# Last three experts' rows added on TensorE by 0/1 matrices, down products three half jobs behind, norm factors split between VectorE and POOL

## What is computed

```python
cap = int(EXPERT_CAPACITY * T / E)                 # 2.0 * 1024 / 8 = 256 tokens an expert
probs = jax.nn.softmax(scores, axis=-1)            # scores = x @ gate_w, 8 experts
top_p, top_idx = jax.lax.top_k(probs_et, cap)      # each expert picks its 256 tokens
xin = jnp.take_along_axis(x[:, None, :, :], top_idx[..., None], axis=2)
h = jax.nn.gelu(jnp.einsum('BElC,ECH->BElH', xin, w1), approximate=False)
y = jnp.einsum('BElH,EHC->BElC', h, w2) * top_p[..., None]
out = jnp.zeros((B, T, C), x.dtype).at[b_idx, top_idx].add(y)
...
x = _layernorm(x + attention(x)); x = _layernorm(x + ffn(x))
```

## Time and profile before

| | before |
|---|---|
| median of 3 runs | 981.73 us (978.76 to 984.08) |
| the profiled execution's own time | 979.79 us |
| its span, first to last instruction | 978.0 us |
| busy: PE, DVE, ACT, POOL | 89%, 73%, 77%, 68% |
| mean granted TensorE clock | 0.956 of full speed |

### The profile page before, as it was taken

How to read it: one execution, slowest core, us unless ns; L and a number is a source line. 1 busy time by engine, 2 the same in 40 slices (tenths; PEclk the granted TensorE clock), 3 DMA queues, 4 the chain that set the end, 5 groups by cost and what they waited for, 6 DMA issues and landing times.

```text
span 978.0 us, 14970 instructions
## 1 busy us (share of the span) xinstructions
PE 870.7 (89%) x4598; PEld 734.7 (75%) x4598; DVE 714.5 (73%) x1178; ACT 749.4 (77%) x1449; POOL 664.1 (68%) x1055
## 2 busy tenths in 40 slices
PE   6899999999999999999999999999998996676550
PEld 4678888888888888888888888777787775575550
DVE  6777777777777777777777777898888865763341
ACT  4988888888888888888988788877787875533441
POOL 4676767677777677767786667666667666756862
PEclk9999999999999999999999999999999997778875
DMA  6000000000000000001020100000000022422424
GB/s 178 2 27 1 28 1 28 1 27 1 28 1 28 1 27 1 28 1 29 0 72 1 28 2 28 4 28 1 17 1 17 1 71 70 122 23 37 85 24 97
DMA packets 48766, 28.57 MB, mean 29 GB/s; under 512 B 5760, under 2 KB 46752, under 8 KB 48688
## 3 DMA queue, kind: packets, MB, share of 16 engines
q1 hardware_dynamic: 43056, 23.29, 8.3%
q0 software_dynamic: 5632, 4.33, 3.3%
HBM read 21.19 MB, written 6.42 MB: 28 GB/s over the span
## 4 chain that ended last, share of the span: by engine, by line
PE 70%; DVE 9%; issue 8%; ACT 5%; POOL 5%; DMA 2%; SPq 1%; POOLq 0%; ACTq 0%; DVEq 0%
PE t_ps L1353 10%; PE ring_b L1316 6%; PE ring_b L1318 6%; PE ring_b L1317 6%; PE ring_a L1316 5%; PE ring_a L1318 5%; PE ring_a L1317 5%; PE u_ps L1316 5%; PE u_ps L1318 5%; PE u_ps L1317 5%; PE o_ps L1316 2%; DVE negmax L916 2%; PE o_ps L1318 2%; PE o_ps L1317 2%; DVE at_lo L923 2%
## 5 line engine op out<-in xcount | busy, mean ns | idle before, releaser
L545 POOL TENSOR_TENSOR attn<-prob 128x1024 f32<-128x1024 f32 x128 | 308.1, 2407 | 192.0 <-ACT prob L688 183.3
L923 DVE TENSOR_TENSOR at_lo<-t_ps,at_hi 128x512 fp32r<-128x512 f32 x253 | 173.7, 687 | 96.5 <-ACT at_hi L671 96.5
L916 DVE TENSOR_REDUCE negmax<-ring_a 128x1 f32<-128x1024 f32 x128 | 156.5, 1222 | 57.3 <-PE ring_a L1318 55.6
L671 ACT ACTIVATE at_hi<-t_ps 128x512 fp32r<-128x512 f32 x253 | 151.4, 598 | 55.5 <-PE t_ps L1353 54.6
L1353 PE MATMUL t_ps<-ident,attn 128*128 128x128 f32 x1012 | 152.8, 273 | 16.6 <-DVE at_lo L923 16.5
L1353 PEld LDWEIGHTS t_ps<-ident,attn 128*128 128x128 f32 x1012 | 123.8, 140 | 45.8 <-DVE at_lo L923 25.8
L916 DVE TENSOR_REDUCE negmax<-ring_b 128x1 f32<-128x1024 f32 x128 | 155.9, 1218 | 1.9 <-PE ring_b L1318 0.9
L688 ACT ACTIVATE prob<-prob,coef 128x1024 f32<-128x1024 f32 x128 | 147.6, 1154 | 2.6 <-POOL coef L516 2.6
L682 ACT ACTIVATE prob<-ring_a,negmax 128x1024 f32<-128x1024 f32 x128 | 142.8, 1115 | 6.3 <-DVE negmax L916 5.8
L682 ACT ACTIVATE prob<-ring_b,negmax 128x1024 f32<-128x1024 f32 x128 | 142.3, 1111 | 1.2 <-DVE negmax L916 1.2
L1316 PE MATMUL ring_b<-xt_hi,q_hi 128*128 128x512 f32 x256 | 111.5, 436 | 2.2 <-ACT prob L682 2.2
(11 more groups left out here) (377 smaller groups left out, 1846.4 us busy)
## 6 DMA issues: line engine op xcount, KB each, us to landing
wq_s<-in_L_attn_Wq SPq DMA_DIRECT2D x16, 128.0 KB, 2.4
wk_s<-in_L_attn_Wk SPq DMA_DIRECT2D x16, 128.0 KB, 2.6
wv_s<-in_L_attn_Wv SPq DMA_DIRECT2D x16, 128.0 KB, 2.1
wvt_s<-in_L_attn_Wv_T SPq DMA_DIRECT2D x16, 128.0 KB, 2.5
wot_s<-in_L_attn_Wo_T SPq DMA_DIRECT2D x16, 128.0 KB, 2.6
raw_a<-in_L_ffn_w SPq DMA_DIRECT2D x8, 256.0 KB
attn<-in_L_ffn_w SPq DMA_DIRECT2D x8, 256.0 KB
xres<-in_L_attn_X SPq DMA_DIRECT2D x2, 512.0 KB, 8.3
```

What stands on the lines that cost most here:

```text
L545: pool.tensor_tensor(attn[:, t % AB, :], prob[:, t % 2, 1, :], prob[:, t % 2, 0, :], ALU.add).then_inc(attn_ready, 1)
L671: act.activation(at_hi[:, g % 2, half * GT:(half + 1) * GT, c], t_bank(t, half)[:, :].rearrange("p (k q) -> p k q", q=P), ACT.Copy).then_i ...
L916: dve.tensor_reduce(negmax[:, par, m:m + 1], ring[m][:, :], axis=AX.X, op=ALU.max, negate=True).then_inc(negmax_ready, 1)
L923: dve.tensor_tensor(at_lo[:, g % 2, k, c], t_bank(t, half)[:, :].rearrange("p (k q) -> p k q", q=P), at_hi[:, g % 2, k, c].bitcast(F32), A ...
```

## The change

1. **Rows by 0/1 matrices.** For the last three jobs (`MIX = 3`: 13, 14, 15) nothing is scattered. POOL writes the numbers 0 to 1023 into a row (`tok_row`, one iota). DVE turns the three experts' indices into floats (`tok_f`) and compares, six passes of 128 x 1024, so that `one_hot[m][k][slot, token]` is 1 where the slot picked the token. PE's `mix(q)` multiplies these by the scaled rows `y_mix`: 16 f32 matmuls of 128 x 128 a job, all three jobs summed up in four PSUM banks that are free by then.
2. **The end of batch 1.** SP's wait counts only the scatters that are left. DVE first adds the two tables (`add_tables`, without a sum), then what PE summed up (`add_mixed`, with the row sum), two tiles to a bank.
3. **Order in a job.** PE does `down(n-3)` in place of `down(n-2)`, and `rows_out` on odd halves; ACT copies `yt` of job q-2 and rounds the next rows ahead of the Gelus, on even halves; DVE does `xs_lower` ahead of `g_lo` on even halves, and scales on odd halves, ahead of `g_lo`.
4. **Norm factors.** DVE computes variance plus eps in one operation on 4 columns (`ln_vars`), POOL only the power (`ln_pows`), in halves, for all norms but the first. Both norms of the second layer stand behind all jobs on ACT, DVE and POOL.

The core of the diff (declarations and the norm functions cut):

```diff
@@ sync
-                    sp.wait_ge(scattered[n], 16 * CT * E // 2 * (b + 1))
+                    sp.wait_ge(scattered[n], 16 * CT * len([q for q in range(E * (b + 1)) if q % 2 == n and not mixes(q)]))
@@ gpsimd
-            ln_factors(1)
+            ln_pows(1, 0)
+            ln_pows(1, 1)
...
+            pool.wait_ge(w_split, 2 * E)
+            pool.iota(tok_row, pattern=[[1, N]], base=0, channel_multiplier=0).then_inc(row_ready, 1)
             for q in range(5):
                 scatter(q)
...
-            for q in range(E, JOBS):
+            for q in range(E, JOBS - MIX):
                 scatter(q)
-                if q == E + 5:
-                    ln_factors(2)
-            ln_factors(3)
+            for n in range(B, 2 * B):
+                for h in range(2):
+                    ln_pows(n, h)
@@ scalar, ffn(n)
+                if half == 0 and 0 <= q - 2 < JOBS:
+                    act.wait_ge(down_ready, q - 1)
+                    need(act, y_ready, q - 3)
+                    act.activation(yt[q % 2], dn_ps, ACT.Copy).then_inc(yt_copied, 1)
...
-                if half == 1 and 0 < q <= JOBS:
-                    act.wait_ge(down_ready, q)
-                    need(act, y_ready, q - 2)
-                    act.activation(yt[(q - 1) % 2], dn_ps, ACT.Copy).then_inc(yt_copied, 1)
@@ vector
+                dve.tensor_scalar(stat[:, 1, c], stat[:, 0, c], 1.0 / D, EPS, ALU.mult, ALU.add).then_inc(ln_var, 1)
...
+            def add_tables(h):
+                dve.wait_ge(x2_in[1][h], 32)
+                s = slice(QT + h * GT, QT + (h + 1) * GT)
+                dve.tensor_tensor(x1[:, s, :], x1[:, s, :], acc_2[1][:, h * GT:(h + 1) * GT, :],
+                                  ALU.add).then_inc(x2_pre, 1)
+            def add_mixed(h):
+                dve.wait_ge(x2_pre, h + 1)
+                for c in range(h * GT, (h + 1) * GT):
+                    j = QT + c
+                    dve.wait_ge(mixed, c // 2 + 1)
+                    dve.scalar_tensor_tensor(out=x1[:, j, :], in0=mix_home(c), scalar=1.0, in1=x1[:, j, :],
+                                             op0=ALU.mult, op1=ALU.add,
+                                             accum_out=rsum[:, j:j + 1]).then_inc(x2_sum, 1)
...
+                for k in range(CT):
+                    dve.tensor_scalar(one_hot[n][k], tok_row, tok_f[:, k, n:n + 1], None,
+                                      ALU.is_equal).then_inc(hot_ready, 1)
@@ vector, ffn(n): rows of job y = q - 2
+                if half == 1 and 0 <= y < JOBS:
+                    dve.wait_ge(y_ready, y + 1)
+                    if not mixes(y):
+                        need(dve, scattered[y % 2], 16 * CT * (y // 2))
+                    dst = y_mix[y - (JOBS - MIX)] if mixes(y) else yr[y % 2]
@@ tensor
+            def mix(q):
+                m = q - (JOBS - MIX)
+                pe.wait_ge(y_scaled, q + 1)
+                pe.wait_ge(hot_ready, CT * (m + 1))
+                for j in range(QT):
+                    for k in range(CT):
+                        last_m = pe.matmul(mix_home(j), one_hot[m][k][:, j * P:(j + 1) * P].bitcast(F32),
+                                           y_mix[m][:, k, :], start=(m == 0 and k == 0 and j % 2 == 0),
+                                           stop=(m == MIX - 1 and k == CT - 1 and j % 2 == 1))
+                    if m == MIX - 1 and j % 2 == 1:
+                        last_m.then_inc(mixed, 1)
...
-                if half == 0 and 0 <= q - 2 < JOBS:
+                if half == 1 and 0 <= q - 2 < JOBS:
                     rows_out(q - 2)
-                if 0 <= n - 2 < 2 * JOBS:
-                    down(n - 2)
+                if 0 <= n - 3 < 2 * JOBS:
+                    down(n - 3)
...
+                if n == 2 * JOBS:
+                    mix(JOBS - 3)
+                if n == 2 * JOBS + 2:
+                    mix(JOBS - 2)
+            mix(JOBS - 1)
```

More of the change, by code:

```diff
@@ L194, in build @@
               for a in (xg0[:, :], flat[:, 4 * N - E * CT * XW:4 * N])]
+        y_mix = [flat[:, n * CAP:(n + 1) * CAP].rearrange("p (k d) -> p k d", d=D) for n in range(MIX)]
+        tok_row = attn[:, 0, :].bitcast(I32)
+        one_hot = [[xt_hi[:, 0:N], xt_hi[:, N:2 * N]], [xt_lo[:, 0:N], xt_lo[:, N:2 * N]],
+                   [t[:, 1].rearrange("p k n -> p (k n)")[:, 2 * N:3 * N] for t in (at_hi, at_lo)]]
+        tok_f = sb("tok_f", [P, CT, MIX])
         pick = sb("pick", [P, CAP], BF16)
@@ L322, in means, with mixes, mix_home @@
             return sum(len(m) for m in MEANS[:n]) + [hi > c for _, hi in MEANS[n]].index(True) + 1
+        def mixes(q):
+            return q >= JOBS - MIX
+        def mix_home(j):
+            return (t_ps, x_ps, u_ps, o_ps)[j // 2][:, (j % 2) * D:(j % 2 + 1) * D]
         def exists(t):
@@ L846, in _ @@
             signs(1, 1)
-            for n in range(14, 2 * JOBS + 2):
+            for n in range(14, 2 * JOBS + 3):
                 ffn(n)
-                if n == 29:
-                    for c in range(QT):
-                        ln_squares(2, c)
+            for c in range(QT):
+                ln_squares(2, c)
             for c in range(QT):
@@ L1144, in ffn @@
                     xs_lower(E)
+                if half == 0 and q + 1 < JOBS and q + 1 != E:
+                    xs_lower(q + 1)
+                y = q - 2
+                if half == 1 and 0 <= y < JOBS:
[3 more added lines that the diff above has]
+                    dst = y_mix[y - (JOBS - MIX)] if mixes(y) else yr[y % 2]
+                    dve.tensor_tensor(dst, yo_ps.rearrange("p (k d) -> p k d", d=D),
+                                      xg[y // E][:, y % E, :, D + y % E:D + y % E + 1].broadcast_to([P, CT, D]),
+                                      ALU.mult).then_inc(y_scaled, 1)
                 if q < JOBS:
@@ L1292, in _ @@
             indices(1, 1)
-            for n in range(14, 28):
+            mix_tokens()
+            for n in range(14, 2 * JOBS):
                 ffn(n)
-            add_parts(2, 0)
-            add_parts(2, 1)
+                if n in (14, 16, 18):
+                    one_hots((n - 14) // 2)
+            add_parts(0)
             ln_means(2, 0)
+            ffn(2 * JOBS + 1)
+            add_parts(1)
             ln_means(2, 1)
-            for n in range(28, 34):
-                ffn(n)
-            ln_end(2, 0)
-            ln_end(2, 1)
-            ffn(34)
-            for h in range(2):
-                add_parts(3, h)
+            ffn(2 * JOBS + 3)
+            ln_vars(2, 0)
+            ln_vars(2, 1)
+            for h in range(2):
+                ln_end(2, h)
+            for h in range(2):
+                add_tables(h)
+            for h in range(2):
+                add_mixed(h)
                 ln_means(3, h)
+            ln_vars(3, 0)
+            ln_vars(3, 1)
             for h in range(2):
@@ L1653, in _ @@
             counts(1, 1)
-            for n in range(15, 2 * JOBS + 3):
+            for n in range(15, 2 * JOBS + 4):
                 ffn(n)
+                if n == 2 * JOBS:
[3 more added lines that the diff above has]
+            mix(JOBS - 1)
 _INS = ["L0_attn_X", "L0_attn_Wq", "L0_attn_Wk", "L0_attn_Wv", "L0_attn_lambda_q1",
```

63 lines of the change are left out of this document (32 added, 31 removed).

## The result

The changed kernel takes **964.63 us** (median of 4 runs, 963.36 to 965.13) beside 980.62 us (4 runs) for the kernel before: ratio 0.983, 95% interval 0.981 to 0.986. The forecast was 963.0, range 957 to 972, faster.

What follows compares the result with a forecast made beforehand. Bounds before: the threshold search to 876 us, POOL from 888.25 to about 943, then POOL's scatters and the final chain. P 883.9, U 933.4, Y 944.1, plus 15.2 gave span 959.3, 18.7 less: 963.0 us, range 957 to 972.

Steps and rivals of the forecast that it cites:

- P: First gather of batch 1, after the threshold search: forecast at 883.9 us on the span, 888.25 before.
- gain and loss: Before the first gather: search 6.1 us shorter; job 4's scaling behind the indices' first half delays gathers from 888.25 to 890.0.
- The rival that the search would not get shorter: Threshold search keeps its length: first gather 6.1 us later, time 969 us; chance 0.14.
- P to the scatter of job 8: Stretch from batch 1's first gather to job 8's scatter, POOL's list unchanged: 33.7 us.
- U: End of the last `up` on PE: P + 48.7, at worst P + 50.3 at half clock; 49.5 taken, 933.4 us.
- the release by the scatter of job 10: Job 12's scaling on DVE begins when job 10's scatter, started at P + 41.2, has landed 5.4 later: P + 46.6.
- Y: End of job 15's scaling, behind three half `down`, two turnings and two mixes: U plus 10.7, 944.1 us.
- The rival of half clock through the mixes: PE at half clock in mixes and last half `down`: 9 us more, time 972 us; chance 0.12.
- unhidden weights: In the mixes each record waits for its own weight load: 31 us more, time 994 us; chance 0.03.
- The end: From Y to the store's end: 6.0 of DVE work, 5.9 of last sums and norm, 3.3 store, sum 15.2 us.
- The edits without a price: Six DVE comparisons of 0.65 to 1.3 us each, the iota, and batch 1's first norm factors: not priced in the forecast.
- where POOL is late they pay nothing: PE's waits for `yt`, 1.4 us a job, go in the new order, but save no time where POOL is late.

Runs made afterwards that it cites:

- Experiment 5: The changed kernel with job 4's rows scaled ahead of the indices of batch 1: 964.11 us, ratio 0.983 to the kernel before.
- experiment 2: The changed kernel with the old order in a job, 0/1 matrices and new norm factors kept: 972.17 us, ratio 0.992 to the kernel before.
- the change's second trace: The changed kernel run once more, unchanged, in a later group: 964.19 us, ratio 0.984 to the kernel before.
- experiment 1: The changed kernel without 0/1 matrices, all rows scattered, new order and norm factors kept: 968.19 us, ratio 0.989 to the kernel before.
- experiment 4: The changed kernel with the old norm factors, three POOL operations on eight columns: 964.99 us, ratio 0.986 to the kernel before.

## Why the prediction was right, point by point

**P.** Forecast 883.9, measured 885.70. Of the 1.8, 1.0 is the later start of the layer in this execution. The other 0.8 is the search: from the first count to P it took 42.1 for 45.6, so 3.5 less, where gain and loss were put at 6.1 and 1.75. Experiment 5 puts the loss at 2.5, and so the gain at 6.0: the term that was mis-sized is the loss. That the gain comes out so near is partly luck: the first three pairs of rounds gave 4.5 where 5.6 was forecast, and the stretch behind them, to the second half of the indices, 1.4 where 0.5 was. The indices' second half came 1.83 behind the first, where it had been 2.30 (887.26 less 884.96 of the earlier trace rows), and the second DMA of job 4's scatter took 1.75 beside the comparisons: 0.47 and 0.2 more to lose. The pairs of rounds went from 9.1, 7.9 and 8.6 to 8.5, 6.6 and 6.0: 6.0 is the forecast's value at the full clock, now with DVE's own work as the floor. The first pair gained only 0.6; in it `cand` waited for POOL, 0.4 longer than before (last section). The rival that the search would not get shorter falls, and experiment 2 shows that it is the order that shortens it.

**P to the scatter of job 8:** forecast 33.7, measured 34.4, and 33.6 in the change's second trace. POOL bounds it as forecast.

**U.** Job 12's scaling began at P + 47.4 (forecast P + 46.6), and not released by a DMA. The scatter of job 10 began at P + 41.9 in place of 41.2, and by the 5.3 that job 8's took from there it was in at P + 47.2; PE and ACT were a little later still. Nor did this scaling set U, though the forecast had it do so. PE's only wait of size from 922 to 938 us is that for job 10's scaling:

```profile
PE ring_b L1677 <- DVE prob L1205: 4.7, 1, 4.7
```

From its end at 925.98 PE ran through into the mixes, first 4 us at half clock (granted 0.50 to 929.9), then at 1.00; in the 10 us up to P + 51 it is 9.98 busy. So PE's own work behind job 10 is the bound there, and the release by the scatter of job 10 is a step that the forecast had wrong. The last `up` ended at 936.1, P + 50.4, near its worst case, which stood for the half clock, and 0.9 over the value taken.

**Y.** Forecast 10.7 behind U, measured 10.3; a matmul cost 0.22 where I took 0.24, at a granted clock of 1.00, that is the full one. The rival of half clock through the mixes falls, and so does that of unhidden weights, the only one that ended slower.

**The end.** Forecast 15.2, measured 15.2 from Y on. Two small errors cancel in it: the last normalising ended 11.3 behind Y where 11.9 was forecast, and the store took 3.9 in place of 3.3. The rest fits, with powers of 1.05 and 1.01 (forecast 1.0), normalising 2.14 (2.2), table adds 1.29 for two (1.3). The tables were asked for at 940.35, P + 54.7, and nobody waited for them.

The edits without a price: the comparisons took 0.75 each and drew out three issues by 0.9 together; the normalising of batch 1's first norm ended 1.1 us later behind the attention, and the first Gelu still came 4.8 us behind the last attention sum, as before.

**What bounds the kernel before: the step that failed.** The prediction had POOL as the bound from 888.25 to 943 and said of PE's waits for `yt` that "where POOL is late they pay nothing". That holds up to job 10. Behind it the old order was the bound, at 5.4 us a job, and experiment 1 shows the new order with all scatters at 3.6. The forecast time did not suffer, since its Y was built from P upward in the new order and took nothing over from the old stretch; my expectation for experiment 2, which did, missed by 3.

**Sum.** The layer from its first count was forecast at 116.7 and took 118.0. Added last, the matrices give 5.7, the order 7.4 and the factors 0.2 us of the layer, together 13.3 of 17.4. The 0.2 is the least sure: behind Y it is 1.3, and the rest of experiment 4's trace happens to be 1.1 shorter. The remaining 4.1 are shared: both the order and the matrices shorten the stretch behind job 10, so that matrices and factors on the old order give 10.0 (experiment 2), order and factors without matrices 11.7 (experiment 1).

## What to carry to other kernels

An engine that is busiest in a stage need not bound all of it: look, item by item, at what releases each piece, and at whether the busy engine itself waits (here POOL did, 5.6 us in three waits). When a long queue is shortened and the order behind it is changed, build the new time up from a point that both share; don't subtract from the old stretch. And compare traces from a common event near the change: here the start of the layer moved by up to 3.6 us between executions, more than some edits were worth.

## What the runs showed of the hardware

**A DVE operation on one column waited a whole GpSimd operation long.** `cand` (128x1, two int32 inputs) takes 0.16 as a rule. In the first rounds it took over 1 us, and ended as the first of POOL's two 128x512 operations did. The change's timelines of DVE and POOL:

```profile
851.00 1.06 DVE L1115 TENSOR_TENSOR cand<-base_j,step 128x1 int32<-128x1 int32 x1
```
```profile
850.76 2.51 POOL L599 TENSOR_TENSOR at_lo<-attn,at_hi 128x512 fp32r<-128x512 f32 x2 [1.02 <-ACT at_hi L748]
```

Two in 2.51, so the first ended at about 852.0, and `cand` at 852.06. In the trace of before the same `cand` took 0.67, since POOL's operation had begun 0.6 ahead of it and not 0.2. The Trainium skill ("SBUF — State Buffer", "Who interferes with whom") has it that a DVE instruction with two inputs in SBUF contends with a GpSimd one that reads SBUF, and that the later one blocks; the trace agrees. It costs 0.9 us in each of the first two rounds of the change, and 0.9 and 0.5 in the kernel before.

**f32 matmuls with new weights at each record** ran 0.22 us apart (two records) for 16 of them in a row: the loads, 0.19 each, stayed hidden.

**POOL's power** took 1.01 to 1.05 for 4 columns and 1.64 to 1.68 for 8.
